# Causal attention with four heads at a time: value products of four heads in one run, row maxima on a written table of steps, loads per head, groups unrolled

## What is computed

```python
q, k, v = (proj(Wq), proj(Wk), proj(Wv))
q = _apply_rope(q, cos, sin)
k = _apply_rope(k, cos, sin)
scores = jnp.einsum('bhqd,bhkd->bhqk', q.astype(jnp.float32), k.astype(jnp.float32)) * scale
scores = jnp.where(causal[None, None], scores, -jnp.inf)
attn = jax.nn.softmax(scores, axis=-1)
out = jnp.einsum('bhqk,bhkd->bhqd', attn, v.astype(jnp.float32))
```

## Time and profile before

| | us |
|---|---|
| median of three runs | 14836.72 (14822.92 to 14843.74) |
| profiled execution, its own time | 14818.84 |
| span in the profile | 14816.9 |
| lead-in and loop of the attention phase | 12913 to 14387 |

### The profile page before, as it was taken

How to read it: one execution, slowest core, us unless ns; L and a number is a source line. 1 busy time by engine, 2 the same in 40 slices (tenths; PEclk the granted TensorE clock), 3 DMA queues, 4 the chain that set the end, 5 groups by cost and what they waited for, 6 DMA issues and landing times. The chain is left out here.

```text
span 14816.9 us, 232336 instructions
## 1 busy us (share of the span) xinstructions
PE 6600.0 (45%) x53605; PEld 4592.0 (31%) x53605; DVE 10244.3 (69%) x54621; ACT 8213.0 (55%) x42324; POOL 866.4 (6%) x824
## 2 busy tenths in 40 slices
PE   6222222222222222222222222246776567688887
PEld 5222222222222222222222222233444344333335
DVE  4777777777777777777777777763853983365551
ACT  4666666666666666666666666652642111133331
POOL 0000000000000000000000000000000861200000
PEclk8555555555555555555555555557996778789999
DMA  1000000000000000000100000000000000201110
GB/s 49 12 18 12 15 16 12 18 12 18 13 18 12 18 12 18 12 18 13 18 13 18 12 18 12 17 8 11 0 1 22 0 0 6 61 10 21 24 19 17
DMA packets 336648, 233.28 MB, mean 16 GB/s; under 512 B 23221, under 2 KB 319873, under 8 KB 335110
## 3 DMA queue, kind: packets, MB, share of 16 engines
q1 hardware_dynamic: 335366, 219.56, 7.9%
HBM read 193.64 MB, written 25.43 MB: 15 GB/s over the span
## 5 line engine op out<-in xcount | busy, mean ns | idle before, releaser
L515 PE MATMUL scan_p_car<-scan_hs,scan_mean_mat 32*32 32x2 f32 x16392 | 578.0, 198 | 6858.6 <-DVE scan_hb L642 6846.2
L515 PEld LDWEIGHTS scan_p_car<-scan_hs,scan_mean_mat 32*32 32x32 f32 x16392 | 402.1, 135 | 7037.5 <-DVE scan_hb L642 7025.0
L560 ACT ACTIVATE scan_act_ps<-scan_act_ps 128x64 f32<-128x64 f32 (+1 forms) x8193 | 1641.7, 200 | 64.6
L560 ACT ACTIVATE scan_act_ps<-scan_r 128x64 f32<-128x64 f32 x2048 | 466.2, 228 | 1869.9 <-DVE scan_r L639 1869.9
L542 PE MATMUL scan_p_y<-scan_c_masked,scan_hb 128*64 128x4 f32 x16384 | 1234.1, 253 | 0.0
L520 PE MATMUL scan_p_car<-scan_eps_row,ones 1*128 1x3 f32 x4102 | 1198.1, 360 | 38.7 <-DMA scan_a_log<-L_attn_a_A_log 38.5
L2378 DVE TENSOR_REDUCE attn_top_pieces<-attn_ps 128x1 f32<-128x512 f32 (+3 forms) x1440 | 824.0, 606 | 563.3 <-PE attn_ps L2261 325.4
L560 ACT ACTIVATE scan_cm<-scan_dl,scan_s 128x64 f32<-128x64 f32 x2049 | 712.1, 348 | 737.4 <-DVE scan_s L665 737.4
L542 PEld LDWEIGHTS scan_p_y<-scan_c_masked,scan_hb 128*64 128x64 f32 x16384 | 1055.4, 216 | 34.8
L639 DVE TENSOR_TENSOR scan_c<-scan_V,scan_cm 128x64 f32<-128x64 f32 x4096 | 739.8, 221 | 460.7 <-ACT scan_cm L560 413.5
L520 PEld LDWEIGHTS scan_p_car<-scan_eps_row,ones 1*128 1x128 f32 x4102 | 1020.2, 307 | 71.5 <-DMA scan_a_log<-L_attn_a_A_log 38.9
(11 more groups left out here) (451 smaller groups left out, 19876.9 us busy)
## 6 DMA issues: line engine op xcount, KB each, us to landing
scan_step_in<-scan_scratch SPq DMA_DIRECT2D x520, 256.0 KB, 6.1
attn_qT<-qk_scratch SPq DMA_DIRECT2D x60, 256.0 KB, 9.3
attn_kT<-qk_scratch SPq DMA_DIRECT2D x60, 256.0 KB, 18.7
qk_scratch<-qkv_parts SPq DMA_DIRECT2D x32, 384.0 KB, 2.5
scan_scratch<-prep_dts SPq DMA_DIRECT2D x32, 256.0 KB, 2.1
x<-L_attn_a_x SPq DMA_DIRECT2D x1, 4096.0 KB
out<-x SPq DMA_DIRECT2D x1, 4096.0 KB
filter_taps<-c_kT SPq DMA_DIRECT2D x1, 2048.0 KB
```

Source lines behind the costliest of these rows:

```text
L515: last = nc.tensor.matmul(p_car[slot][rows, 0:2], mean_mat[rows, :], hs[rows, :], start=False, stop=True)
L560: nc.scalar.activation(dst, src, func, **kw).then_inc(counts[par]["act"], 1)
```

## The change

In the loop over steps the four value products of a step are issued in one run (`values(it, n)`), with no piece between the pairs; those of a group's last step come after the scores of the next group's step 0. Pieces stand on steps 2 to 35 by a table (`spread`) that deals out their cost (width + 128) by the number of queries in the step. A piece on the diagonal is one matmul and the mask instead of up to two and the mask, and so are the scores. In the lead-in one unit is a whole row of up to 2048 keys over four banks, with one maximum: 64 instead of 160. The loads are per head (12 transfers of 64 KB), each with its own semaphore; heads 1 to 3 of group `it + 1` are asked for four steps before their first piece, head 0 of group `it + 2` after the last scores of group `it`. The groups are unrolled; nothing is loaded or computed beyond group 7. `top_transposed` comes at step 36 instead of 37. The masks are loaded after group 0.

```diff
-    FIRST_STEP, PER_STEP = 4, 5
+    FIRST_STEP, LAST_STEP = 2, 35
+    def spread():
+
+        room = sum(queries(n) for n in range(FIRST_STEP, LAST_STEP + 1))
+        cost = [piece_width(u) + P for u in range(len(PIECES))]
+        found, u, due = {n: [] for n in range(len(STEPS))}, 0, 0.0
+        for n in range(FIRST_STEP, LAST_STEP + 1):
+            due += queries(n) / room * sum(cost)
+            while u < len(PIECES) and (sum(cost[:u]) + cost[u] / 2 < due or n == LAST_STEP):
+                found[n].append(u)
+                u += 1
+        return found
...
+                for h in range(HG):
+                    load(0, h)
                 for k in range(2):
                     sp.dma_start(mask_in[:, k, :], ins["c_causal"][k]).then_inc(loaded, 16)
-                sp.sem_inc(top_in, 16)
-                load(0, 0)
-                load(1, 1)
-                move_rows(0, 0)
-                with sp.Fori(0, GROUPS // 2) as i:
-                    for s in range(2):
-                        it = i * 2 + s
-                        move_rows(1 - s, it + 1)
-                        sp.wait_ge(pv_done, (it + 1) * len(STEPS) + 1)
-                        load(s, (it + 2) % GROUPS)
+                load(1, 0)
+                move_rows(0)
+                for it in range(GROUPS):
+                    if it + 1 < GROUPS:
+                        for h in range(1, HG):
+                            sp.wait_ge(s_done, it * STEP_PAIRS + 2 * (FIRST_OF_HEAD[h] - FETCH_AHEAD))
+                            load(it + 1, h)
+                        move_rows(it + 1)
+                    if it + 2 < GROUPS:
+                        sp.wait_ge(s_done, (it + 1) * STEP_PAIRS)
+                        load(it + 2, 0)
...
-                            for pair in range(2):
-                                scores(it, s, n, pair)
-                                for u in pieces[1 * pair:1 + 1 * pair]:
-                                    piece(it + 1, 1 - s, u)
-                            for pair in range(2):
-                                if n:
-                                    values(it, s, n - 1, pair)
-                                for u in pieces[2 + 1 * pair:3 + 2 * pair]:
-                                    piece(it + 1, 1 - s, u)
+                for it in range(GROUPS):
+                    pe.wait_ge(top_in, (it + 1) * (PARTS * 16))
+                    for n, (c, kt) in enumerate(STEPS):
+                        found, chunk = FOUND[n] if it + 1 < GROUPS else [], it * CHUNKS + c
+                        places = [[u for k, u in enumerate(found) if 4 * k // len(found) == place] for place in range(4)]
+                        scores(it, n, 0)
+                        for u in places[0]:
+                            piece(it + 1, u)
+                        scores(it, n, 1)
+                        for u in places[1]:
+                            piece(it + 1, u)
+                        if n:
+                            values(it, n - 1)
+                        elif it:
+                            values(it - 1, len(STEPS) - 1)
+                        for u in places[2] + places[3]:
+                            piece(it + 1, u)
...
+                def unit_maximum(u):
+
+                    j = u % TB
+                    dve.wait_ge(score_done, u + 1)
+                    found = ps[:, 4 * (u % 2):4 * (u % 2) + 4, :].rearrange("p k t -> p (k t)")
+                    nc.vector.tensor_reduce(out=top_pieces[:, u, 0:1], in_=found[:, 0:(j + 1) * P], axis=AX.X, op=ALU.max).then_inc(max_done, 1)
```

More of the change, by code:

```diff
@@ L2183, in _, with load @@
             def _(sp):
+                def load(it, h):
+                    s, b, first = it % 2, it // (GROUPS // B), (it % (GROUPS // B) * HG + h) * HD
+                    for w, dst in enumerate((qT[s], kT[s])):
+                        for n, term in enumerate(TERMS):
+                            src = scratch[w, b:b + 1, term[w], first:first + HD, :].rearrange("o d t -> d o t")
+                            sp.dma_start(dst[n * HD:(n + 1) * HD, h:h + 1, :], src).then_inc(qk_in[s][h], 16)
@@ L2184, in _, with move_rows @@
+                def move_rows(it):
+                    sp.wait_ge(top_copied, it + 1)
+                    for r in range(PARTS):
+                        sp.dma_start(qT[it % 2][ROWS + r:ROWS + r + 1, :, :].rearrange("o h t -> o (h t)"), top_rows[:, r, :]).then_inc(top_in, 16)
+                for h in range(HG):
+                    load(0, h)
                 for k in range(2):
                     sp.dma_start(mask_in[:, k, :], ins["c_causal"][k]).then_inc(loaded, 16)
[L2187 to L2194, removed]
@@ L2268, in top_transposed, with scores @@
                     last.then_inc(top_t, 1)
-                def scores(it, s, n, pair):
+                def scores(it, n, pair):
                     c, kt = STEPS[n]
[L2273 to L2277, removed]
+                    off, s = max(kt - GP * c, 0) * P, it % 2
+                    if it or n:
+                        pe.wait_ge(exp_done, it * STEP_PAIRS + 2 * n + pair - 1)
+                    for h in (2 * pair, 2 * pair + 1):
+                        dst = ps[:, h, :]
@@ L2287, in scores, with values @@
                     last.then_inc(s_done, 1)
-                def values(it, s, n, pair):
+                def values(it, n):
                     c, kt = STEPS[n]
[L2292 to L2297, removed]
+                    off, chunk = max(kt - GP * c, 0) * P, it * CHUNKS + c
+                    pe.wait_ge(exp_done, it * STEP_PAIRS + 2 * n + 2)
+                    if n == 0:
+                        pe.wait_ge(v_in, it + 1)
+                    if kt == 0 and chunk >= 2:
+                        pe.wait_ge(divided, chunk - 1)
+                    for h in range(HG):
+                        last = nc.tensor.matmul(ps[h * VW:(h + 1) * VW, SUM_BANK + c % 2, off:], vs[it % 2][:, kt, h, :], pT[(2 * n + h // 2) % 4][:, h % 2, off:],
@@ L2307, in turned @@
                     last.then_inc(o_t, 1)
[L2309 to L2311 removed]
+                for u in range(UNITS):
+                    unit(u)
                 top_transposed(0)
[L2313 to L2322, removed]
[L2323 to L2338 removed]
@@ new lines, in _ @@
+                for it in range(GROUPS):
[15 more added lines that the diff above has]
+                            piece(it + 1, u)
+                        if chunk and kt == 2:
+                            turned(chunk - 1)
+                        if n == LAST_STEP + 1 and it + 1 < GROUPS:
+                            top_transposed(it + 1)
@@ L2340, in _ @@
+                values(GROUPS - 1, len(STEPS) - 1)
+                turned(GROUPS * CHUNKS - 1)
             @block.scalar
```

190 lines of the change are left out of this document (92 added, 98 removed).

## The result

The changed kernel takes 14455.3 us (median; 14439.8 to 14458.4), the kernel before 14840.2 us beside it (14822.9 to 14847.6): a ratio of 0.974, 95% interval 0.9723 to 0.9757. The forecast was 14440, the range 14345 to 14540. The profiled execution took 14455.84 us (span 14454.1). In the trace the attention phase, from the first to the last instruction of its code, fell from 1524.9 to 1134.1 us: 391 less, where the sum said 393.

The account below looks back on a forecast made before the run. TensorE was taken to set the loop's pace, broken by waits for maxima and loads. Loop 346 us, lead-in 23 and end 24 less make 393, giving 14426 or 14444 by baseline; forecast 14440, range 14345 to 14540.

Parts of the forecast that it names:

- The sum: Attention phase: loop 1012 us (346 less), lead-in 23 less, end 24 less, together 393 us less.
- Value products together: Full steps: four heads' value products issue in about one pair's time, 1.10 us less issue, of which 0.6 arrives.
- The walk of a full step: Loop: issue and two-bank waits followed through one step; 3.75 us with five wide pieces, 3.6 with the actual widths.
- the term for six pieces: Nine full steps per group hold six pieces, 4.1 us each, 36.9 us in all.
- the term for the starts of chunks: Three full steps per group with short values but a 0.68 us VectorE copy: 11.7 us.
- Last group: Loop's end: without its 160 unused maxima, the last group takes about 81 us.
- Loads per head: Group changes: about 130 us of stalls shrink to six head-0 waits of 3.0 us, 18 us in all.
- Lead-in: Before the loop: 64 wide maxima gain 26.6 us (0.12k + 0.27 per k-block unit), first matmul 3.4 later; net 23.
- 1 (maxima hidden, 14332): Full steps: VectorE's maxima overlap, so a step is 3.1 us as issued, 108 us less; chance 0.12.
- 2 (the exchange takes all): Full steps: the two-bank ping-pong holds the step at 4.25 us, 80 us more, 14520; chance 0.15.
- 3 and 4 (code behind data): Loop: code late behind 27 head loads, 14720, chance 0.06; or unrolled code waited for throughout, up to 15480, chance 0.02.
- The last sign of being wrong: Loop: the prediction is wrong if TensorE's clock falls to 1.2 GHz there; it was 0.94 of full before.

Follow-up runs that it names:

- c1_after_again: The changed kernel run and traced a second time with nothing altered; 14435.7 us, 0.973 of the kernel before.

## Why the prediction was right

**The sum.** Loop 1015.8 for 1012, which is 342.7 less for 346; lead-in with its start 24.2 less for 23; end 24.0 less for 24: 391 for 393. The loop's 3.8 us over the forecast are 1.4 less of groups' own work (7 x 129.8 for 7 x 130), 3.7 less of waits (14.3 for 18), 2.0 less in the last group, and about 11 more of clock: 8.9 behind the waits and 2.0 in steps 0 and 1 of group 0, which run at a granted clock of 0.50 and take 6.3 us for 4.3 in the other groups. The sum had no term for the clock. The remaining 15 us to the median lie inside the scatter of the unchanged phases.

**Value products together.** Right, with the size a little low: of the 1.1 us, 0.6 was to arrive in a full step, and 0.67 (pairs) to 0.72 (the kernel before) do. 1.00 us for four column groups of 512 held beside pieces. The Trainium skill (TensorE: Matmul & The Clock Gate, section on packing small matmuls) gives 2.38 times for three column tiles; here four cost what two do, so the 50 us estimated from that figure did not come.

**The walk of a full step.** Five pieces: 3.66 us in the mean of 13 steps for 3.6; four: 2.99 for 3.1; six: 4.49 in the mean of nine for 4.1. What failed is the term for six pieces: forecast from the widths in them, they take more than the walk's bound for six wide ones (4.33). All 23 steps make 90.9 us for 86.8, and three of the four sets of transposes, priced at 2.8 beside them, are in the 90.9. The rest is offset where the term for the starts of chunks was too high: steps 4, 12 and 24 take 9.8 us for 11.7. The other steps came as summed (29.1 us, with the waits and the clock taken off, for 28.8). So that 129.8 us stand against 130 is partly luck.

**Last group.** 79.8 us for 81, and 2.2 for the 3 of the last transposes and division. In the kernel before this group took 175.2 us, 19.2 of them a wait for loads. No run puts its 160 unused maxima back alone.

**Loads per head.** 2.4 us of wait in the mean for 3.0. At the first turn the first issue is at 13163.29, TensorE stops at 13168.57 and goes on at 13171.76: 5.3 and 8.5 us after the issue, for 5.2 and 8.2. What the sum left out is the clock, 1.5 us a group. The prediction priced the group changes at 130 us; loads per group in the changed kernel bring back 126. That the new code has no branch is worth nothing by itself, which the prediction did not see: it listed the branch's stalls as a cost of their own, beside the load waits. The Trainium skill (DMA: Bandwidth & Descriptors, its table of what to do) says to coalesce many small transfers and calls those under 64 KB mostly overhead. The ones here are at that bound, and twelve of 256 KB in place of 48 of 64 KB lose 126 us: the first piece needs head 0 alone, and waits 21.5 to 22.9 us when it lands with the other three.

**Lead-in.** The maxima give 22.6 us for 26.6. The formula for a unit was at fault: the mean of both engines' work, 0.12k + 0.27, gives 2.19 us for 16 blocks, less than the 2.29 us that the maximum alone takes. VectorE paces this part, with 80.5 us of maxima and 6.0 idle, and from the first matmul to the start of the split (13026.10) it is 86.7 us for 82.6. The first matmul comes 1.6 us earlier, not 3.4 later: the masks' issue at 22.4 us does hold it (25.2 us after the phase's start), but the kernel before waited for the loads of all four heads of group 0 and started at 26.9. The two errors, 4.0 and 5.0 us, nearly cancel: 24.2 for 23.

**End.** 24.0 us as forecast.

**Rivals.** 1 (maxima hidden, 14332) did not happen. The third bank, which takes away nearly all of TensorE's waits for maxima, brings about its price (113 us for 108, 14326), though a full step is then 3.33 us and not 3.1. 2 (the exchange takes all) is true of steps with six pieces alone. 3 and 4 (code behind data) did not happen: no wait over 0.8 us on TensorE's weight loads or matmuls in the loop is put down to issue. The last sign of being wrong, a fall to 1.2 GHz in the loop, did come, behind five of the six short waits and in group 0's first steps; its 11 us are few beside the 391.

## What to carry to other kernels

Issue small matmuls of different column groups in one run: here two heads took 0.99 us and four took 1.00. When such a gain arrives only in part, look for a two-bank exchange and find it a third bank, here worth 113 us for a list of which slot each product takes. Before you remove a stall, ask what runs behind it: here the stall at the loop's branch hid loads, and removing it alone gained nothing.

## What the runs showed of the hardware

- TensorE's clock fell behind waits of 1.9 to 3.2 us, shorter than I had thought would matter: in the changed kernel the granted clock was 0.50 to 0.72 in the six us behind five of the six head-0 waits, and 1.00 behind the shortest, of 1.63 us. The length of the wait alone does not decide it. Behind 1.63 and 2.10 us:

```profile
13574.30:13580.30 6.00, 5.93 (x60) 3.19 (x61) 4.40 (x10) 2.83 (x5) 0.00 (x0) 1.00 0.01 3
13706.20:13712.20 6.00, 5.94 (x46) 3.49 (x47) 3.22 (x7) 1.36 (x3) 0.00 (x0) 0.72 0.01 3
```

and in the second trace of the same kernel (c1_after_again) behind 2.11 and 1.90 us, where it is the shorter one that lowers the clock. What separates the two these traces do not show:

```profile
13689.60:13695.60 6.00, 5.92 (x60) 3.19 (x61) 4.40 (x10) 2.83 (x5) 0.00 (x0) 1.00 0.01 3
13821.40:13827.40 6.00, 6.00 (x46) 3.10 (x47) 3.22 (x7) 1.38 (x4) 0.00 (x0) 0.72 0.01 4
```

- A maximum over 2048 columns in four PSUM banks takes 2.29 us as one instruction, four of 512 take 2.52.
